# A graph layer on one core: gathers of 127 rows instead of 128, chunks of 508 edges

## The chip, the cores and the metric

The kernel runs on one core of a Trainium2 chip. A core has five engines that run their own instruction streams and meet at semaphores: TensorE (PE), VectorE (DVE), ScalarE (ACT), GpSimd (POOL) and SyncE (SP, which here only starts transfers). Sixteen DMA engines move data between the chip's memory (HBM) and the on-chip memory (SBUF, 128 partitions, called lanes here). The metric is the device time of one execution in microseconds.

## The reference, cut to what matters

One layer of a graph network on N = 6250 nodes of D = 256 features and E = 200000 edges, sorted by their destination node `dst`. The part that the change touches is the attention over the edges:

```python
xw = (x @ W).reshape(N, H, C)                  # H = 8 heads of C = 32
e = leaky_relu(a_src[src] + a_dst[dst], 0.2)
ex = exp(e - m[dst])                           # m: a bound per destination
denom = segment_sum(ex, dst, N)
msg = xw[src] * (ex / denom[dst])[:, :, None]
out = relu(segment_sum(msg, dst, N) + bias)
```

Beside it stand a second attention over all nodes (the "mix" part) and, behind both, a layer of 16 experts of which each node takes two.

## The kernel before

**Stages.** A setup (0 to about 50 us) builds tables; a keys stage (to about 370 us) goes over the nodes in 50 tiles of 128 and writes one row of ROW = 264 floats per node to the HBM tensor `node_rows` (its projected features and its 8 source logits); the edge loop (to about 3180 us) handles the edges; the experts and the last normalization follow.

**Chunks and steps.** The edges are cut into chunks of CHUNK = 512: four tiles of 128 edges, one edge per lane. The destinations are cut into 49 blocks of 128 nodes. A step handles one chunk against one block; since the edges are sorted, a chunk that reaches over a block's end is taken once more with the next block. That makes STEPS = CHUNKS + BLOCKS - 1 = 392 + 48 = 440 steps. Which chunk and block belong to a step is computed in the setup (`blk_row`, `need_row`, `first_row`).

**GpSimd** gathers. `gather` (line 205) starts four indirect transfers per chunk; each takes 128 rows of `node_rows`, one into each lane of `rows_g`, at the row numbers in `idx`. `rows_g` holds R = 4 chunks. Before a chunk's buffer is filled again, GpSimd waits on `msg_ready` for the last step that reads it (`last_use`, line 960). **SP** waits for each chunk's landing, counts it in `chunks_in` (line 985), and every four chunks loads their row numbers from `src_lists` into `idx` (line 215).

**VectorE**, in each step: builds the 0/1 matrix `sel` (line 1083), adds up the destination logits `ends` (1144), waits for the chunk and forms the logits `lg` (1150 to 1154), adds the sums of two steps ago from `p_m` to `acc` (1092), and multiplies the gathered features with the weights into `msg` (1161). **ScalarE** takes the exponentials (1059, 1061) and builds the matrix `sel_t` for three steps ahead (1011, 1014) out of `dst_all`, which an ACT-issued transfer fills for four steps at a time (222). **TensorE** spreads the destination logits (1183) and sums the messages per node (1193). Between these, the mix part runs as "query" work, spread over the steps (lines 1019 to 1037 on ScalarE, 1201 to 1252 on TensorE). The loop is unrolled on all of these engines.

**The lists.** `src_lists[p, chunk, u]` is the source node of the edge at lane p of tile u. SP writes it from `src` in 48 transfers of 8 chunks each during the keys stage (line 847), the last chunks in the setup (337 to 341). `dst_pad` is `dst` with padding, one row per chunk; `d_bf` are its rows per step, minus the block's first node, turned so that the lane is the inner index; an edge of another block or a padded one matches no node of the block.

Of the kernel before, what the change touches and what calls it, by code (L numbers as in the profile page):

```python
# [19 lines left out]
P = 128  # L20
N = 6250
E = 200000
# [8 lines left out]
CHUNK = TILES_PER_CHUNK * P  # L31
CHUNKS = 392
STEPS = CHUNKS + BLOCKS - 1
# [40 lines left out]
assert STEPS % OCT == 0 and GROUPS_Q * SPAN + OCT < STEPS and OCT % R == 0  # L74
assert LIST_TILES % 2 == 0 and LIST_TILES * LIST_CHUNKS <= E // CHUNK and CHUNKS % (2 * R) == 0 and CHUNKS * CHUNK >= E and CHUNKS == OCT * (T - 1)

# [54 lines left out]
def gps_layer(nc, x, src, dst, gnn_W, att_src, att_dst, gnn_bias, Wqkv, bqkv, Wproj, bproj, temperature,  # L131
# [12 lines left out]
    with top:  # L144
# [5 lines left out]
        dst_bc = nc.dram_tensor("dst_bc", (4 * P, CHUNK), BF16).ap()  # L150
# [85 lines left out]
        with ExitStack() as c:  # L236
# [29 lines left out]
            d_bf = [sb(f"d_bf{i}", [P, CHUNK], BF16, ctx=c) for i in range(G4)]  # L266
# [51 lines left out]
            def _(sp):  # L318
                full = E // CHUNK
                rest = E - full * CHUNK  # L320
                sp.dma_start(fd[:, 0:full], dst[0:full * CHUNK].rearrange("(c b) -> c b", b=CHUNK)[:, 0:1].rearrange("c a -> a c"),
                             allow_slow_non_contiguous=True).then_inc(first_in, 16)
                sp.dma_start(fd[:, full:full + 1], dst[full * CHUNK:full * CHUNK + 1].unsqueeze(0)).then_inc(first_in, 16)
                sp.dma_start(dst_pad[0:full, :], dst[0:full * CHUNK].rearrange("(a b) -> a b", b=CHUNK)).then_inc(dst_padded, 16)
# [14 lines left out]
                sp.dma_start(src_lists[:, lo:full, :], src[lo * CHUNK:full * CHUNK].rearrange("(a p u) -> p a u", p=P, u=u4)).then_inc(scratch_out, 16)  # L339
# [15 lines left out]
                sp.wait_ge(scratch_out, (2 + TQ - T + G4 + 1) * 16)  # L355

            @block.gpsimd
            def _(pool):
# [14 lines left out]
                pool.wait_ge(dst_padded, 4 * 16)  # L373
# [5 lines left out]
            def _(dve):  # L379
                dve.memset(resid[:, NFULL:T, :], 0.0).then_inc(x_zeroed, 1)  # L380
                dve.memset(att_bd[:], 0.0).then_inc(att_zeroed, 1)
                dve.memset(pad_s[:], 0).then_inc(pads_set, 1)
                dve.memset(pad_i[:], PAD_DST).then_inc(pads_set, 1)
# [26 lines left out]
                dve.wait_ge(first_in, 2 * 16)  # L410
# [132 lines left out]
        with ExitStack() as c:  # L543
# [1470 lines left out]
```

## Time and profile before

| | us |
|---|---|
| time, median of two runs | 3901.03 (3893.41 and 3908.66) |
| span of the profiled execution | 3964.1 |
| PE busy | 2866.8 (72%) |
| DVE busy | 2138.6 (54%) |
| POOL busy | 1990.0 (50%) |
| ACT busy | 1439.2 (36%) |
| software DMA queue (GpSimd's transfers) | 21.8% of 16 engines |

The profile is that of one execution. "Busy" counts the time in which an engine works on instructions other than register, branch, semaphore and transfer-starting ones; an indirect transfer on GpSimd counts, since GpSimd writes its list of pieces itself. "Idle before" a group of instructions is the engine's idle time just ahead of them, with the instruction whose semaphore ended it; "issue" means that the profile shows nothing that was waited for, and "remote" that the semaphore's writer is not among the records. A transfer's own time on the DMA engines is not part of the instruction that starts it.

### The profile page before, as it was taken

How to read it: one execution, taken by the hardware profiler on the slowest of the kernel's cores; microseconds unless marked ns; L12 is line 12 of the kernel's file. 1: busy time of each engine (PE TensorE's matmuls, PEld its weight loads, DVE VectorE, ACT ScalarE, POOL GpSimd, SP SyncE). 2: the span in 40 equal slices, each digit the busy share in tenths (PEclk: the TensorE clock that was granted, in tenths of full speed). 3: DMA queues.
4: the chain of work that ended last, by engine and by line, in shares of the span. 5: the costliest groups of instructions: out<-in, count | busy, mean ns of one | idle time of the engine just before them, and what ended most of it. 6: DMA issues, size and time to landing. Idle time of an engine off the chain costs nothing. (4 is left out here: it accounts for less than half of the span.)

```text
span 3964.1 us, 53285 instructions
## 1 busy us (share of the span) xinstructions
PE 2866.8 (72%) x12200; PEld 1793.8 (45%) x12200; DVE 2138.6 (54%) x5047; ACT 1439.2 (36%) x3425; POOL 1990.0 (50%) x2097
## 2 busy tenths in 40 slices
PE   5998776768677767676767675867685442599997
PEld 3554343434344333434343333333443332488885
DVE  7888545555555554545555555554555584333335
ACT  3444433334333334343434343433343221122226
POOL 3666554555555555555555555555555445222223
PEclk9999787878778788777877788878778755799999
DMA  5222333333333333333333333333333312677776
GB/s 140 44 44 62 108 97 92 100 101 101 101 102 106 96 105 99 105 97 105 97 96 97 109 93 104 99 104 99 98 96 105 89 39 82 205 233 232 233 232 222
DMA packets 298730, 453.14 MB, mean 114 GB/s; under 512 B 117295, under 2 KB 193348, under 8 KB 298479
## 3 DMA queue, kind: packets, MB, share of 16 engines
q0 software_dynamic: 86608, 243.35, 21.8%
q1 hardware_dynamic: 184143, 135.80, 12.5%
q10 hardware_dynamic: 27744, 71.38, 5.3%
q8 instruction: 83, 1.36, 0.1%
q14 instruction: 152, 1.25, 0.1%
HBM read 395.09 MB, written 56.88 MB: 114 GB/s over the span
## 5 line engine op out<-in xcount | busy, mean ns | idle before, releaser
L211 POOL DMA_INDIRECT rows_g<-node_rows,idx x1568 | 1488.3, 949 | 1293.4 <-DVE msg L1161 829.8
L1193 PE MATMUL p_m<-msg,sel 128*128 128x264 f32 x3520 | 1114.1, 469 | 292.5 <-DVE msg L1161 185.0
L1193 PEld LDWEIGHTS p_m<-msg,sel 128*128 128x128 f32 x3520 | 769.9, 230 | 447.7 <-issue 308.0
L1161 DVE TENSOR_TENSOR msg<-rows_g,p_w 128x1024 f32<-128x1024 f32 x440 | 536.2, 1219 | 345.6 <-ACT p_w L1059 228.9
L1037 ACT ACTIVATE qfeat<-p_scr 128x512 f32<-128x512 f32 x442 | 245.0, 593 | 798.9 <-remote 603.2
L1216 PE MATMUL p_scr<-q_t,sel_sum 32*128 32x512 f32 x832 | 340.9, 774 | 221.0 <-ACT qfeat L1037 177.1
L1083 DVE TENSOR_TENSOR sel<-p_w,dst_t 128x512 f32<-128x512 f32 x441 | 304.3, 690 | 139.0 <-issue 114.9
L1092 DVE TENSOR_TENSOR acc<-acc,p_m 128x264 f32 x440 | 189.0, 429 | 311.4 <-remote 280.6
L1014 ACT ACTIVATE sel_t<-apart,ones 128x512 bf16<-128x512 bf16 x443 | 319.7, 722 | 31.3 <-issue 1.1
L1011 ACT ACTIVATE apart<-dst_all,iota_neg 128x512 bf16<-128x512 bf16 x443 | 314.1, 709 | 0.0
L1845 POOL DMA_INDIRECT moe<-ysb,token x128 | 123.7, 966 | 379.2 <-DVE ysb L1834 354.9
L1059 ACT ACTIVATE p_w<-lg 128x32 f32<-128x32 f32 x440 | 88.4, 201 | 575.2 <-DVE lg L1154 451.7
L1183 PEld LDWEIGHTS p_sp<-adm_parts,sel_t 128*128 128x128 bf16 x1768 | 99.7, 103 | 428.4 <-issue 419.3
L1216 PEld LDWEIGHTS p_scr<-q_t,sel_sum 32*128 32x128 f32 x832 | 97.9, 219 | 367.2 <-issue 331.4
L1800 ACT ACTIVATE ht<-e_ph,ba 128x256 f32<-128x256 f32 x256 | 100.3, 474 | 415.7 <-PE e_ph L1770 409.9
L1770 PE MATMUL e_ph<-xst,wa 128*128 128x256 f32 x1024 | 234.0, 382 | 3.6 <-DMA bb<-in_L_ffn_b_dram 1.9
L1224 PE MATMUL p_y<-qfeat,mix_w 128*32 128x512 f32 x832 | 170.7, 686 | 88.3 <-ACT qfeat L1037 73.8
L540 POOL TENSOR_TENSOR acc<-kk 128x512 f32<-128x512 f32 x150 | 167.7, 1147 | 131.2 <-DVE kk L773 131.2
L1779 PE MATMUL e_py<-wb,ht 128*128 128x256 f32 x1024 | 231.4, 379 | 0.0
L1144 DVE TENSOR_REDUCE ends<-p_sp 128x64 f32<-128x192 f32 x440 | 153.6, 349 | 136.5 <-remote 119.7
L1183 PE MATMUL p_sp<-adm_parts,sel_t 128*128 x1768 | 127.8, 193 | 115.0 <-DVE lg L1154 80.8
L1770 PEld LDWEIGHTS e_ph<-xst,wa 128*128 128x128 f32 x1024 | 195.8, 192 | 31.9 <-issue 5.0
(328 smaller groups left out, 3375.6 us busy)
## 6 DMA issues: line engine op xcount, KB each, us to landing
dst_all<-dst_bc ACTq DMA_DIRECT2D x112, 512.0 KB
wa<-in_L_ffn_w_dram SPq DMA_DIRECT2D x64, 512.0 KB
wb<-in_L_ffn_w_dram SPq DMA_DIRECT2D x64, 512.0 KB
rows_g<-node_rows,idx POOLq DMA_INDIRECT x1568
xs<-slot_x SPq DMA_DIRECT2D x64, 258.0 KB
ya<-moe SPq DMA_DIRECT2D x48, 256.0 KB, 4.3
bb<-in_L_ffn_b_dram SPq DMA_DIRECT2D x64, 128.0 KB
qs<-xn_turned ACTq DMA_DIRECT2D x13, 512.0 KB
```

Source lines behind the costliest of these rows:

```text
L211: pool.indirect_dma_start(rows_g[:, j, u, :], None, node_rows, bass.IndirectOffsetOnAxis(ap=idx[q][:, j, u:u + 1], axis=0)).then_inc(gathe ...
L1011: act.activation(apart[j % 2][:], dst_all[q][:, j, :], ACT.Square, bias=iota_neg[:])
L1014: act.activation(sel_t[j][:], apart[j % 2][:], ACT.Relu, bias=ones[:, 0:1], scale=-1.0).then_inc(sel_t_ready, 1)
L1037: act.activation(feat[slot(name)][:], bank(name)[:], ACT.Square).then_inc(act_freed, 1)
L1083: dve.tensor_tensor(sel[j][:], p_w[:, P:2 * P].unsqueeze(1).broadcast_to([P, TC, P]), d.unsqueeze(2).broadcast_to([P, TC, P]), ALU.is_equa ...
L1092: dve.tensor_tensor(a, a, p_m[j % 2][:, 0:ROW], ALU.add).then_inc(acc_added, 1)
L1161: dve.tensor_tensor(m4, g3[:, :, 0:D].rearrange("p u (h e) -> p u h e", h=H), p_w[:, 0:TC * H].rearrange("p (u h) -> p u h", u=TC).unsquee ...
L1183: mm = pe.matmul(p_e(j)[:, u * 6 * H:(u + 1) * 6 * H], sel_t[j][:, u * P:(u + 1) * P], adm_parts[:, bass.ds(b, 1), :, :].rearrange("p a r ...
L1193: mm = pe.matmul(p_m[j % 2][:, 0:ROW], sel[j][:, u, :], msg[j % 2][:, u, :], start=(u == 0), stop=(u == TC - 1))
L1216: pe.matmul(bank(name)[:], sel_sum[rows, m * P:(m + 1) * P], q_t[g][rows, :], start=True, stop=True).then_inc(act_filled, 1)
L1770: mm = pe.matmul(p_h[s % 2][:, m * SLOT_ROWS:(m + 1) * SLOT_ROWS], wa[s][:, k, m * P:(m + 1) * P], xst[s % 2][:, k, :], start=(k == 0), st ...
L1779: mm = pe.matmul(p_y[s % 2][:, a * D:(a + 1) * D], ht[s % 2][:, k, a * P:(a + 1) * P], wb[s][:, k, :], start=(k == 0), stop=(k == KF - 1))
```

## The change

An indirect transfer takes 127 rows into lanes 0 to 126; lane 127 carries no edge. A chunk has four tiles of 127 edges, 508 in all, so the 200000 edges fill 394 chunks (FILLED; tables and lists are laid out for CHUNKS = 396), and there are 394 + 48 = 442 steps. Everything else in a step keeps its 128 lanes. Lane 127 has its own values: its destinations are NO_DST = -64, which matches no node, its row numbers are 0, and the lanes 96 to 127 of `rows_g` are set to zero once at the start of the keys stage. The loops on GpSimd and SP now end at chunk 394 and not at a multiple of 8. The lists are written with the chunk as outer index, and transfers over 393 full chunks are cut in two, at 384.

```diff
-CHUNK = TILES_PER_CHUNK * P
-CHUNKS = 392
-STEPS = CHUNKS + BLOCKS - 1
+LANES = 127
+CHUNK = TILES_PER_CHUNK * LANES
+FILLED = -(-E // CHUNK)
+CHUNKS = 396
+STEPS = FILLED + BLOCKS - 1
+WIDE = TILES_PER_CHUNK * P
+NO_DST = -64.0
...
             for u in range(TC):
-                pool.indirect_dma_start(rows_g[:, j, u, :], None, node_rows,
-                                        bass.IndirectOffsetOnAxis(ap=idx[q][:, j, u:u + 1], axis=0)).then_inc(gathered[j], 16)
+                pool.indirect_dma_start(rows_g[0:LANES, j, u, :], None, node_rows,
+                                        bass.IndirectOffsetOnAxis(ap=idx[q][0:LANES, j, u:u + 1], axis=0)).then_inc(gathered[j], 16)
...
+                even = full - full % 16
+                for lo, hi in ((0, even), (even, full)):
+                    sp.dma_start(fd[:, lo:hi], dst[lo * CHUNK:hi * CHUNK].rearrange("(c b) -> c b", b=CHUNK)[:, 0:1].rearrange("c a -> a c"),
+                                 allow_slow_non_contiguous=True).then_inc(first_in, 16)
...
+                for p in range(LANES, P):
+                    sp.dma_start(src_lists[p:p + 1, 0:full, :].rearrange("p a u -> p (a u)").rearrange("p (a b) -> (p a) b", a=u4),
+                                 pad_s[0:u4, 0:full]).then_inc(scratch_out, 16)
...
+                for g in range(G4):
+                    dve.memset(d_bf[g][:], NO_DST)
...
-                    dve.tensor_scalar(d_bf[g][:].rearrange("c (u p) -> c u p", u=TILES_PER_CHUNK),
+                    dve.tensor_scalar(d_bf[g][:].rearrange("c (u p) -> c u p", u=TILES_PER_CHUNK)[:, :, 0:LANES],
...
                 dve.memset(zeros[:], 0.0)
+                dve.memset(rows_g[P - C:P].rearrange("p r u f -> p (r u f)"), 0.0)
...
-                    sp.dma_start(src_lists[:, bass.ts(t, LIST_CHUNKS), :],
-                                 src[bass.ts(t, LIST_CHUNKS * CHUNK)].rearrange("(a p u) -> p a u", p=P, u=TILES_PER_CHUNK)).then_inc(lists_out, 16)
+                    sp.dma_start(src_lists[0:LANES, bass.ts(t, LIST_CHUNKS), :].rearrange("p a u -> a p u"),
+                                 src[bass.ts(t, LIST_CHUNKS * CHUNK)].rearrange("(a p u) -> a p u", p=LANES, u=TILES_PER_CHUNK)).then_inc(lists_out, 16)
```

On GpSimd, the place where the keys stage ends and the edge loop begins, before (three chunks are gathered ahead of the loop, then groups of four with a table lookup for each):

```order
L211 DMA rows_g<-node_rows,idx 128x264 x12
L543 UNCONDITIONAL_BRANCH
L958 UNCONDITIONAL_BRANCH
L211 DMA rows_g<-node_rows,idx 128x264 x4
L962 TENSOR_LOAD tables
L962 ISA x2
```

And the same place now:

```order
L215 DMA rows_g<-node_rows,idx 127x264 x12
L556 UNCONDITIONAL_BRANCH
L972 UNCONDITIONAL_BRANCH
L215 DMA rows_g<-node_rows,idx 127x264 x4
L976 TENSOR_LOAD tables
L976 ISA x2
```

Nothing has moved there; each transfer has 127 rows of 264 floats. On SP, the first transfers of the setup before, up to the last list:

```order
L321 DMA fd<-in_dst_dram 1x390x1
L323 DMA fd<-in_dst_dram 1x1
L324 DMA dst_pad<-in_dst_dram 16x12480
L325 DMA dst_pad<-in_dst_dram 16x20
L327 DMA dst_pad<-pad_i 1x192
L328 DMA dst_pad<-pad_i 1x512
L332 DMA resid<-in_x_dram 128x12x256 x4
L334 DMA resid<-in_x_dram 106x256
L337 DMA src_lists<-pad_s 128x8
L339 DMA src_lists<-in_src_dram 128x6x4
L341 DMA src_lists<-in_src_dram 80x4
```

And the same place now:

```order
L327 DMA fd<-in_dst_dram 1x384x1
L327 DMA fd<-in_dst_dram 1x9x1
L329 DMA fd<-in_dst_dram 1x1
L331 DMA dst_pad<-in_dst_dram 16x12192
L331 DMA dst_pad<-in_dst_dram 12x381
L332 DMA dst_pad<-in_dst_dram 4x89
L334 DMA dst_pad<-pad_i 1x152
L335 DMA dst_pad<-pad_i 2x508
L339 DMA resid<-in_x_dram 128x12x256 x4
L341 DMA resid<-in_x_dram 106x256
L344 DMA src_lists<-pad_s 128x12
L346 DMA src_lists<-in_src_dram 9x127x4
```

There are three more transfers in the setup, two of them in these rows and one for lane 127 of the lists behind them, and the lists' outer index is now the chunk.

## Rows read from the trace of the kernel before

**Rows 1.** The page, 40 equal slices of the span, busy tenths.

```profile
PE   5998776768677767676767675867685442599997
DVE  7888545555555554545555555554555584333335
POOL 3666554555555555555555555555555445222223
DMA  5222333333333333333333333333333312677776
```

**Rows 2.** Busy time in two stretches (clock, DMA share, GB/s last).

```profile
100.00:360.00 260.00, 255.38 (x1406) 134.56 (x1402) 223.96 (x537) 126.33 (x413) 180.53 (x206) 1.00 0.24 45
...
500.00:3100.00 2600.00, 1826.12 (x7130) 1031.74 (x7130) 1377.51 (x3020) 996.52 (x2216) 1386.14 (x1462) 0.80 0.35 100
```

**Rows 3.** By source line: ns min/median/max, first and last start in us.

```profile
L211 POOL DMA_INDIRECT rows_g<-node_rows,idx x1568: 940/946/1413, 376.0 to 3156.6; - x196
...
L1161 DVE TENSOR_TENSOR msg<-rows_g,p_w x440: 1206/1220/1223, 400.9 to 3172.8; 128x1024 f32<-128x1024 f32 x147
```

**Rows 4.** The page, costliest groups: busy us, mean ns, idle before.

```profile
L211 POOL DMA_INDIRECT rows_g<-node_rows,idx x1568 | 1488.3, 949 | 1293.4 <-DVE msg L1161 829.8
```

**Rows 5.** Timeline of two pauses (start, length, idle before).

```profile
1848.25 0.94 POOL L211 DMA_INDIRECT rows_g<-node_rows,idx  x1 [0.30 <-issue]
1849.50 0.95 POOL L211 DMA_INDIRECT rows_g<-node_rows,idx  x1 [0.30 <-issue]
...
1853.85 0.69 DVE L1083 TENSOR_TENSOR sel<-p_w,dst_t 128x512 f32<-128x512 f32 x1 [6.71 <-issue]
...
1854.51 0.95 POOL L211 DMA_INDIRECT rows_g<-node_rows,idx  x1 [0.30 <-issue]
1858.14 0.19 DVE L1150 TENSOR_TENSOR lg<-rows_g,ends 128x32 f32<-128x32 f32 x1 [3.34 <-issue]
1858.21 1.08 ACT L1037 ACTIVATE qfeat<-p_scr 128x512 f32<-128x512 f32 x2 [11.60 <-remote]
...
1898.79 0.95 POOL L211 DMA_INDIRECT rows_g<-node_rows,idx  x1 [0.30 <-issue]
1902.14 0.69 ACT L1030 ACTIVATE r_norm<-p_scr,c_col 128x512 f32<-128x512 f32 x1 [10.77 <-remote]
```

**Rows 6.** Waits of the whole span: us in total, times, longest.

```profile
POOL rows_g L211 <- DVE msg L1161: 829.8, 186, 10.8
```

**Rows 7.** Timeline of two undisturbed steps on VectorE.

```profile
1790.11 1.21 DVE L1161 TENSOR_TENSOR msg<-rows_g,p_w 128x1024 f32<-128x1024 f32 x1
...
1793.69 1.22 DVE L1161 TENSOR_TENSOR msg<-rows_g,p_w 128x1024 f32<-128x1024 f32 x1
```

**Rows 8.** Windows of 2 us at the second pause.

```profile
1899.00:1901.00 2.00, 0.00 (x0) 0.00 (x0) 0.02 (x1) 0.00 (x0) 0.74 (x1) 0.50 0.50 133
1901.00:1903.00 2.00, 0.12 (x1) 0.12 (x1) 0.00 (x0) 0.78 (x2) 0.00 (x0) 0.50 0.01 2
```

**Rows 9.** Register instructions of VectorE's sequencer, by source line.

```profile
L1150 DVEq ALU_OP  x880: 1/45/1422, 398.4 to 3171.3; - x176
...
L1139 DVEq SEQ_ASSERT  x440: 5/23/729, 395.5 to 3170.2; - x147
```

**Rows 10.** Transfers that GpSimd starts, with their counts.

```profile
rows_g<-node_rows,idx POOLq DMA_INDIRECT x1568
...
moe<-ysb,token POOLq DMA_INDIRECT x128
...
slot_x<-acc,places POOLq DMA_INDIRECT x98
...
d_rows<-dst_pad,cidx POOLq DMA_INDIRECT x4, 6.5
```

**Rows 11.** The software queue: packets, MB, share of 16 engines.

```profile
q0 software_dynamic: 86608, 243.35, 21.8%
```

**Rows 12.** Two memsets of VectorE, by source line.

```profile
L382 DVE MEMSET pad_s<- x1: 485/485/485, 1.6 to 1.6; 128x512 int32 x1
...
L407 DVE MEMSET acc<- x1: 4232/4232/4232, 6.6 to 6.6; 128x5008 f32 x1
```

**Rows 13.** VectorE at the setup's end and the keys stage's start.

```profile
46.86 0.17 DVE L463 TENSOR_SCALAR t_col<-t_col 128x2 f32<-128x2 f32 x1 [3.81 <-DMA bq_col<-in_L_mix_bqkv_dram]
...
58.51 0.15 DVE L750 COPY mask<-vmask 128x1 f32<-128x1 f32 x1 [1.39 <-PE p_kv L689]
```

**Rows 14.** The list transfers: issue times, and landing.

```profile
L847 SPq DMA_DIRECT2D src_lists<-in_src_dram x48: 585/622/1592, 59.5 to 355.1; - x48
...
DMA to landing us min/median/max: 5.8/6.7/8.6
```

More of the change, by code:

```diff
@@ L73 @@
 WEIGH_STEPS = ((7, 9, 12, 15), (19, 21, 23, 25))
-assert STEPS % OCT == 0 and GROUPS_Q * SPAN + OCT < STEPS and OCT % R == 0
-assert LIST_TILES % 2 == 0 and LIST_TILES * LIST_CHUNKS <= E // CHUNK and CHUNKS % (2 * R) == 0 and CHUNKS * CHUNK >= E and CHUNKS == OCT * (T - 1)
+assert GROUPS_Q * SPAN + OCT < STEPS and OCT % R == 0
+assert LIST_TILES % 2 == 0 and LIST_TILES * LIST_CHUNKS <= E // CHUNK and CHUNKS % R == 0 and CHUNKS - R < FILLED < CHUNKS and STEPS + 2 * R <= 4 * P
 def wait(eng, sem, value):
@@ L265, in gps_layer @@
             ident_bf = sb("ident_bf", [P, P], BF16, ctx=c)
-            d_bf = [sb(f"d_bf{i}", [P, CHUNK], BF16, ctx=c) for i in range(G4)]
+            d_bf = [sb(f"d_bf{i}", [P, WIDE], BF16, ctx=c) for i in range(G4)]
             p_g = ps("p_g", [P, 512], c)
@@ L320, in _ @@
                 rest = E - full * CHUNK
-                sp.dma_start(fd[:, 0:full], dst[0:full * CHUNK].rearrange("(c b) -> c b", b=CHUNK)[:, 0:1].rearrange("c a -> a c"),
-                             allow_slow_non_contiguous=True).then_inc(first_in, 16)
+                even = full - full % 16
+                for lo, hi in ((0, even), (even, full)):
+                    sp.dma_start(fd[:, lo:hi], dst[lo * CHUNK:hi * CHUNK].rearrange("(c b) -> c b", b=CHUNK)[:, 0:1].rearrange("c a -> a c"),
+                                 allow_slow_non_contiguous=True).then_inc(first_in, 16)
                 sp.dma_start(fd[:, full:full + 1], dst[full * CHUNK:full * CHUNK + 1].unsqueeze(0)).then_inc(first_in, 16)
-                sp.dma_start(dst_pad[0:full, :], dst[0:full * CHUNK].rearrange("(a b) -> a b", b=CHUNK)).then_inc(dst_padded, 16)
+                for lo, hi in ((0, even), (even, full)):
+                    sp.dma_start(dst_pad[lo:hi, :], dst[lo * CHUNK:hi * CHUNK].rearrange("(a b) -> a b", b=CHUNK)).then_inc(dst_padded, 16)
                 sp.dma_start(dst_pad[full:full + 1, 0:rest], dst[full * CHUNK:E].unsqueeze(0)).then_inc(dst_padded, 16)
@@ L974, in _ @@
                     body(R + j, 1, j, done[j])
-                for i in range(1, CHUNKS // (2 * R)):
-                    for q in range(2):
-                        done = [last_use(i * (2 * R) + q * R + j) for j in range(R)]
-                        for j in range(R):
-                            body(i * (2 * R) + q * R + j, q, j, done[j])
+                for i in range(2, CHUNKS // R):
+                    js = range(min(R, FILLED - i * R))
+                    done = [last_use(i * R + j) for j in js]
+                    for j in js:
+                        body(i * R + j, i % 2, j, done[j])
             @block.sync
@@ L985, in arrived @@
                     sp.sem_inc(chunks_in, 1)
-                def body(ch, q, more):
-                    for j in range(R):
+                for ch in range(0, CHUNKS, R):
+                    for j in range(min(R, FILLED - ch)):
                         arrived(ch + j, j)
-                    if more:
-                        fetch_lists(sp, ch + 2 * R, q)
-                body(0, 0, True)
-                body(R, 1, True)
-                for i in range(1, CHUNKS // (2 * R) - 1):
-                    for q in range(2):
-                        body(i * (2 * R) + q * R, q, True)
-                for q in range(2):
-                    body(CHUNKS - (2 - q) * R, q, False)
+                    if ch + 2 * R < CHUNKS:
+                        fetch_lists(sp, ch + 2 * R, ch // R % 2)
             @block.scalar
@@ L1073, in _ @@
                 for q in range(2):
-                    act.wait_ge(dst_in[q], (STEPS // R // 2 + 1) * 16)
+                    act.wait_ge(dst_in[q], (1 + len(range(1 + q * R, STEPS, 2 * R))) * 16)
                 act.wait_ge(q_in, GROUPS_Q * 16)
```

11 lines of the change are left out of this document (6 added, 5 removed).

## Prediction, made before the changed kernel ran

> **What bounds the kernel now.** I read the 40 slices of the page first [rows 1], then the busy time in two long windows [rows 2]. From 500 to 3100 us no engine is full: TensorE is busy 0.70 of the time, VectorE 0.53, GpSimd 0.53, ScalarE 0.38, and the DMA engines 0.35. The keys stage (100 to 360 us) is different: PE is busy 0.98 of it. So the loop over steps waits on something, and it takes most of the program: the 440 multiplies `msg` of line 1161 start from 400.9 to 3172.8 us [rows 3], 6.3 us per step.
>
> GpSimd's account explains the length of the loop. It starts its 1568 gathers from 376.0 to 3156.6 us, 2781 us [rows 3]. One gather occupies it 0.949 us on average [rows 4], and back to back they start 1.25 us apart (1848.25 to 1849.50 us in [rows 5]), so a chunk of four costs 5.0 us and all of them 1568 x 1.25 = 1960 us. The rest is waiting for `msg` to free a buffer: 829.8 us in 186 waits, the longest 10.8 us [rows 6]. 1960 + 830 = 2790 us, the loop to within 0.4%. So loop = gathers x 1.25 + W, where W is what GpSimd waits for the other engines.
>
> Are the other engines slow by their own work? No. Two successive `msg` start 3.6 us apart when nothing disturbs them (1790.11 and 1793.69 us, [rows 7]), less than the 5.0 us of a chunk. W comes from pauses. In [rows 5] GpSimd runs seven gathers without a break while ScalarE does nothing for 11.60 us and VectorE waits 6.71 us with "issue" as releaser, which means that no semaphore explains it. Both go on at 1858.14 and 1858.21 us, 2.7 us after the end of the last gather's issue (1854.51 + 0.95). The second pause reads the same: last gather 1898.79 + 0.95 = 1899.74 us, ScalarE back at 1902.14 us after 10.77 us. The windows beside it show why I connect the two: DMA share 0.50 from 1899 to 1901 us, 0.01 from 1901 to 1903 us, and the engines come back in the quiet window [rows 8]. VectorE's sequencer shows it from inside: register instructions of line 1150 with a median of 45 ns take up to 1422 ns, an assertion of 23 ns up to 729 ns [rows 9]. Something that every sequencer needs is withheld while gathers are in flight, and is given back when GpSimd has filled its four chunk buffers and must stop. I do not know from these rows what it is; I only use when it ends.
>
> **What a gather does to the DMA engines.** The software queue moved 86608 packets for 1568 + 128 + 98 + 4 indirect transfers and 3 plain ones [rows 10, 11], 48 packets for each: 3 for each of 16 engines. So 128 rows are split evenly, 8 to an engine, and all 16 engines serve every gather at once.
>
> **The change, part by part.**
> 1. 127 rows instead of 128. 127 is prime; if the split must stay even, all rows go to one engine. Price of the transfer: the queue's 243.35 MB took 21.8% of 16 engines' span [rows 11], 0.218 x 16 x 3964 = 13826 us, 17.6 KB per us of one engine. 127 rows of 1056 bytes are 134 KB, 7.6 us on one engine, where sixteenths take about 0.5 us. Hidden: a buffer is refilled in 5.0 us of issue, lands at most 7.6 us later, and is read by about 3.6 us of step, 16.2 us against the 4 x 5.0 = 20 us that four buffers give. The cover is 3.8 us; if the engines serve a gather slower than 11 us, VectorE waits for rows.
> 2. What it does to the pauses. No row shows a gather that uses one engine, so W is bounded from both sides: 0 if the pauses go, 830 if nothing changes, and 830 + 186 x 7 = 2130 if each wait lasts as long as the longer tail of the last gather. I take half of W, 415 us. The reason for a gain rather than a loss: a pause needs traffic that keeps all 16 DMA engines supplied from GpSimd; with one engine per gather about six of sixteen are in use (7.6 / 1.25), and whatever the sequencers fetch or write has free engines in between. The reason for only half: the DMA engines are idle for two thirds of the loop already (share 0.35), and the gaps between two gathers don't end a pause now, so it is not a matter of full DMA engines alone.
> 3. GpSimd's issue of one gather. It covers the same number of rows, so I take 1.25 us. Bounds by the nearest rows: 0.940 to 1.413 us busy for gathers of this kind [rows 3], so -0.01 to +0.46 us on each of 1576, -10 to +730 us; I take the median because 1568 of them agree with it.
> 4. Size. 1576 gathers instead of 1568: +10 us. Two more steps without query work: already inside the formula, since loop = gathers x 1.25 + W; as steps they would be 2 x 6.3 = 12.6 us with pauses, 2 x 3.6 without. I take +10 for both.
> 5. Setup. Four more memsets of 128x512 on VectorE, at most 485 ns each (the 4-byte one of line 382, [rows 12]), +1.9 us; hidden in part by the 3.81 us that VectorE waits for `bq_col` [rows 13], but SP then issues three more transfers of 0.4 to 0.6 us in that same stretch. +2 us together. The memset of lanes 96 to 127 of `rows_g` is 4224 elements long; 5008 took 4232 ns [rows 12], so 3.6 us, at the place where VectorE waits only 1.39 us for the first projection [rows 13]: +2.2 us.
> 6. Source lists. 48 transfers are cut 8 x 127 x 4 instead of 128 x 8 x 4, so on 8 engines instead of 16 and about twice as long. Now one lands 6.7 us after issue [rows 14]; doubled it is 13.4 us against a whole stage of about 300 us, and only `fetch_lists` at its end waits for them. The last one starts at 355.1 us and the first gather at 376.0 us [rows 3, 14], so 20.9 - 6.7 = 14 us cover the extra 6.7 us. 0 us; without that cover +7 us.
>
> Sum: -415 + 10 + 2 + 2 = -401 us. The profiled execution has a span of 3964 us, the two timed runs 3893 and 3909 us with a median of 3901; the profiled one is 1.6% longer, and I carry the difference over: 3964 - 401 = 3563 us of span, 3500 us timed.
>
> Here a page speaks for point 1. The Trainium skill, "DMA: Bandwidth & Descriptors", section "Why a DMA increments its semaphore by 16 and not by 1", says that a transfer runs on the largest number of engines up to 16 that divides its outermost dimension, and gives 127 partitions as the case with one; on GpSimd's queue successive transfers move round the engines. The same section lists an exception, direct copies from GpSimd that spread 127 partitions over all 16. The trace agrees with the even split of 128 (48 packets each) and shows neither case for 127.
>
> **The rivals.**
> - Nothing changes (the split stays on 16 engines, or moves and the pauses don't care). For: 7 or 8 rows per engine is an easy split, and the pauses may hang on the number of rows in flight. W stays 830: 3901 + 14 = 3915 us. The exception named above would give this.
> - Slower, longer pauses. For: in both pauses shown the engines return only after the traffic has stopped, and on one engine it stops up to 7 us later. It decides against the change as soon as the pauses do not thin out. The waits have a mean of 4.5 us and a longest of 10.8; my estimate is that some 70 of the 186 are long ones of 6 us and more, and if these grow by 7 us each it is +490 us, 4400 us.
> - Slower, the issue. For: writing 127 rows' worth of descriptors for one engine may be serial. From 1.25 + 830/1576 = 1.78 us per gather on, GpSimd alone makes the loop as long as now, whatever the pauses do. At 2.5 us: 3940 us of loop, +1150, 5050 us. Against: no indirect transfer in the trace, of rows of 1 to 2 KB, takes more than about 1.4 us.
> - All gathers on the same engine: 1576 x 7.6 = 11980 us. Only if the engine were fixed; the trace has no sign of one.
>
> **How the numbers follow.** One engine and thinner pauses 0.43 (3500 us, its own range 3090 to 3820: W gone or nearly kept); one engine, pauses as now 0.09; still 16 engines 0.17 (both 3915 us); longer pauses 0.20 (3915 to 4400 us, of which a quarter below 3980); dearer issue 0.10 (3700 to 5050 us); fixed engine 0.01. The range 3090 to 4400 us leaves out about 0.15. A measurement of this kernel can tell about 2% from no change, so faster means below 3823 us: 0.43 + 0.02 = 0.45. Within 2%: 0.09 + 0.17 = 0.26 less what drifts out, plus the small end of the longer pauses, 0.25. Slower: 0.30.
>
> **What would show it.** Step 1: packets per gather and the time from the end of issue to landing; if a chunk still arrives 1 to 2 us after its last issue, all 16 engines serve it. Step 2: GpSimd's wait for `msg`, 415 us; 829.8 again means the pauses stay, over 1200 the tail matters. Step 3: mean of the gather's busy time, 0.95 us; above 1.4 us the issue has become the bound, and the wait for `msg` would vanish. Steps 5 and 6: the keys stage starts at most 5 us later and lasts as long as before. I am wrong from the ground up if the waits vanish and the loop is not shorter, or if VectorE's `lg` starts to wait for rows.

## Result, and the profile after

The changed kernel takes 5773.04 us (median of two runs, 5769.27 and 5776.81), against 3901.03 us before: a ratio of 1.479, 95% interval 1.470 to 1.487. The prediction was 3500 us with a range of 3090 to 4400 us. The time lies outside it, on the other side of no change.

The profiled execution of after has a span of 5775.0 us. In the table below, all of the growth is in the edge loop.

| us | before | after |
|---|---|---|
| span | 3964.1 | 5775.0 |
| first gather starts | 376.0 | 378.1 |
| first to last gather | 2780.6 | 4606.7 |
| from the last gather's start to the end | 807.5 | 790.2 |
| gathers | 1568 | 1576 |
| GpSimd busy with one gather | 0.949 | 2.541 |
| GpSimd's wait for `msg` | 829.8 | 17.0 |

The page of after, 40 slices (answers to [rows 1]); GpSimd now stands at 8 tenths through the whole loop, and VectorE fell from 5 tenths to 3:

```profile
PE   6975545455555555455555545555555543348998
DVE  8863333333333333333323332332323233553334
POOL 4778888888888888888888888888888888662223
DMA  4223333323233333333333333333333333227776
```

The same stretch as the second row of [rows 2], with the same columns:

```profile
500.00:3100.00 2600.00, 1392.10 (x4391) 787.84 (x4390) 832.42 (x1843) 606.88 (x1358) 2262.06 (x891) 0.67 0.31 64
```

GpSimd is busy 2262 of 2600 us (before: 1386) and does 891 things in that time where it did 1462. The gather by its source line, its group on the page, and the software queue (answers to [rows 3, 4, 11]):

```profile
L215 POOL DMA_INDIRECT rows_g<-node_rows,idx x1576: 2530/2540/2952, 378.1 to 4984.8; - x197
...
L215 POOL DMA_INDIRECT rows_g<-node_rows,idx x1576 | 4004.1, 2541 | 605.3 <-issue 588.3
...
q0 software_dynamic: 843408, 254.77, 22.4%
```

No gather takes less than 2.53 us. The queue's packets went from 86608 [rows 11] to 843408. The 230 other indirect transfers keep about 48 each, so a 127-row gather has (843408 - 230 x 48) / 1576 = 528 packets instead of 48. The waits of the whole span (answers to [rows 6]):

```profile
DVE lg L1156 <- SPq L999: 2814.4, 391, 11.0
...
POOL rows_g L215 <- DVE msg L1167: 17.0, 23, 1.1
```

The roles have changed. GpSimd hardly waits for `msg` any more (17.0 us instead of 829.8), and VectorE waits 2814.4 us for rows to arrive. The loop is GpSimd's own work: (4004.1 + 605.3 - 17.0) / 1576 = 2.914 us per gather, 1576 x 2.914 = 4592 us, plus the 17.

What became of the pauses is in VectorE's register instructions at `lg`, where [rows 9] had 1422 ns as the maximum:

```profile
L1156 DVEq ALU_OP  x884: 40/45/52, 424.4 to 4995.7; - x177
```

From 1 to 1422 ns around the median of 45 the spread has shrunk to 40 to 52. The stall inside the sequencers is gone. So half of the prediction came true, and something else, larger, went wrong.

The start of the gathers in the timeline of after says whether the 2.54 us are GpSimd's own:

```profile
378.12 2.63 POOL L215 DMA_INDIRECT rows_g<-node_rows,idx  x1 [0.18 <-issue]
381.06 2.54 POOL L215 DMA_INDIRECT rows_g<-node_rows,idx  x1 [0.30 <-issue]
```

The first gather of the program takes 2.63 us with no other gather in flight. It isn't held back by the ones before it.

### The profile page after: what moved, and what is told of

Read it like the earlier page. It is cut to its first block and busy times, and to the rows that moved or that the text cites. A ratio compares the mean times of both kernels' runs of the same rounds, so it can differ in the third digit from the quotient of the medians.

```text
span 5775.0 us, 53429 instructions
## 1 busy us (share of the span) xinstructions
PE 3339.7 (58%) x12224; PEld 2068.9 (36%) x12224; DVE 2139.6 (37%) x5066; ACT 1435.7 (25%) x3433; POOL 4507.9 (78%) x2105
## 2 busy tenths in 40 slices
DMA packets 1055435, 465.10 MB, mean 81 GB/s; under 512 B 873663, under 2 KB 949734, under 8 KB 1055184
## 3 DMA queue, kind: packets, MB, share of 16 engines
q0 software_dynamic: 843408, 254.77, 22.4%
q14 instruction: 152, 1.25, 0.1%
## 5 line engine op out<-in xcount | busy, mean ns | idle before, releaser
L215 POOL DMA_INDIRECT rows_g<-node_rows,idx x1576 | 4004.1, 2541 | 605.3 <-issue 588.3
L1199 PE MATMUL p_m<-msg,sel 128*128 128x264 f32 x3536 | 1539.4, 609 | 513.7 <-DVE msg L1167 505.9
L1199 PEld LDWEIGHTS p_m<-msg,sel 128*128 128x128 f32 x3536 | 1027.3, 305 | 791.1 <-issue 549.2
L1156 DVE TENSOR_TENSOR lg<-rows_g,ends 128x32 f32<-128x32 f32 x442 | 84.9, 192 | 2832.7 <-SPq L999 2814.4
L1189 PE MATMUL p_sp<-adm_parts,sel_t 128*128 x1776 | 140.5, 206 | 1506.7 <-DVE lg L1160 1477.4
L1222 PE MATMUL p_scr<-q_t,sel_sum 32*128 32x512 f32 x832 | 325.9, 780 | 102.2 <-DVE q_gram L1118 102.2
L1785 PEld LDWEIGHTS e_py<-wb,ht 128*128 128x128 f32 x1024 | 189.7, 190 | 23.2
```

Source lines behind the costliest of these rows:

```text
L215: pool.indirect_dma_start(rows_g[0:LANES, j, u, :], None, node_rows, bass.IndirectOffsetOnAxis(ap=idx[q][0:LANES, j, u:u + 1], axis=0)).th ...
L1189: mm = pe.matmul(p_e(j)[:, u * 6 * H:(u + 1) * 6 * H], sel_t[j][:, u * P:(u + 1) * P], adm_parts[:, bass.ds(b, 1), :, :].rearrange("p a r ...
L1199: mm = pe.matmul(p_m[j % 2][:, 0:ROW], sel[j][:, u, :], msg[j % 2][:, u, :], start=(u == 0), stop=(u == TC - 1))
L1222: pe.matmul(bank(name)[:], sel_sum[rows, m * P:(m + 1) * P], q_t[g][rows, :], start=True, stop=True).then_inc(act_filled, 1)
L1785: mm = pe.matmul(p_y[s % 2][:, a * D:(a + 1) * D], ht[s % 2][:, k, a * P:(a + 1) * P], wb[s][:, k, :], start=(k == 0), stop=(k == KF - 1))
```

## The experiments

In the diffs below a line with - is of the kernel named, and only the lines that matter are shown. Two theories of the loss were open (the row count by itself, or something else in the change), then three rules for how the row count acts, and then two for the pauses: K, they need a gather on (nearly) all 16 engines, as the prediction said; and P, they need gathers that follow each other closely, at 1.25 us or little more.

### The row count alone, and everything but the row count

**e1**, from the kernel before:

```diff
+GATHER = 127
...
-                pool.indirect_dma_start(rows_g[:, j, u, :], None, node_rows,
+                pool.indirect_dma_start(rows_g[0:GATHER, j, u, :], None, node_rows,
```

> The kernel before (chunks of 512 edges, 440 steps, lists as before); only the gathers take 127 rows, and lanes 96 to 127 of rows_g are zeroed once. The 128th edge of each tile is left out. Theory (the gather's row count is the whole cause): the gather stays busy 2.54 us and starts 2.84 us apart, the loop takes 1568 x 2.92 = 4580 us, total 5700 to 5770 us. Rival (the cause lies in the new lists, the new chunk size or the lane-127 data): the gather goes back to 0.95 us and the total to 3900 to 3950 us.

**e2**, from the changed kernel:

```diff
-                pool.indirect_dma_start(rows_g[0:LANES, j, u, :], None, node_rows,
+                pool.indirect_dma_start(rows_g[:, j, u, :], None, node_rows,
```

> The changed kernel (chunks of 508, 442 steps, new lists and setup) with the gather alone put back to 128 rows; lane 127 then fetches row 0 of node_rows, which matches no destination. Theory (the row count is the whole cause): gather busy 0.95 us, pauses and wait for msg as before (830 us, give or take 60), total 3901 + 14 = 3915 us, ratio 1.00 to 1.01. Rival (the rest of the change costs something by itself): above 3960 us, with a longer keys stage or a longer wait for idx.

e1 took 5750.2 us (one run; before on the same chip 3905.9), e2 3927.7 us, a ratio of 1.006 (1.004 to 1.008). Their groups on the page, e1 first:

```profile
L212 POOL DMA_INDIRECT rows_g<-node_rows,idx x1568 | 3987.9, 2543 | 597.0 <-issue 585.1
```

```profile
L215 POOL DMA_INDIRECT rows_g<-node_rows,idx x1576 | 1496.2, 949 | 1254.0 <-DVE msg L1167 785.9
```

One row less in each gather makes up 1844 of the 1872 us lost. Chunks of 508, two more steps, the new lists and the setup cost 22 us together (0.6%).

### How the row count acts

**e3, e4, e5 and e6** are e1 with 124, 122, 126 and 120 in the place of 127. Like e1 they leave out edges (those of the missing lanes), so they measure time only; the steps and the number of gathers are those of the kernel before.

> The kernel before with gathers of 124 rows (4 x 31); the last four edges of each tile are left out. Theory A: a gather uses the largest number of engines up to 16 that divides its rows (4 engines, 31 rows each, 8 packets of up to 4 rows) and every one of the 16 queues gets as many entries as the fullest, 8 x 16 = 128; issue time is linear in entries between the two cases measured (32 entries 0.949 us, 512 entries 2.541 us): 1.27 us busy, 1.57 us apart, 2460 us for all, plus what GpSimd waits for msg: total 3570 us if the pauses go, 3990 us if half of them stay, 4400 us if all stay. Theory B: every count that is not a multiple of 16 is written row by row at about 20 ns a row: 2.48 us busy, total 5600 us. Theory C (only prime or odd counts are special): as before, 0.93 us busy, total 3900 us.

> The kernel before with gathers of 122 rows (2 x 61); the last six edges of each tile are left out. Theory A (largest divisor up to 16, here 2; 61 rows on each, 16 packets, 256 entries): 1.69 us busy, 1.99 us apart, 3120 us for all plus the wait for msg: total 4230 us if the pauses are gone, up to 4700 if half stay. Theory B (all counts that are no multiple of 16 alike): 2.44 us busy, total 5500 us. Theory C (only odd counts): 0.92 us, total 3900 us.

> The kernel before with gathers of 126 rows (14 x 9); the last two edges of each tile are left out. Entries by the divisor rule: 14 engines, 9 rows each, 3 packets, 3 x 16 = 48 entries (blank ones on two engines only), issue 0.95 to 1.0 us, 1.30 us apart, 2040 us for all. Theory K (the pauses need a gather on all 16 engines; 4 engines had none): the wait for msg nearly vanishes, the loop is 2040 to 2150 us, total 3150 to 3300 us. Rival P (the pauses were thinned by the slower pace of 1.6 us and not by fewer engines): wait for msg about 800 us as before, total 3850 to 3950 us.

> The kernel before with gathers of 120 rows (15 x 8); the last eight edges of each tile are left out. Entries by the divisor rule: 15 engines, 8 rows each, 2 packets, 32 entries, so the issue time is that of 128 rows, 0.95 us (a cost per row would give 0.89). Theory K (pauses need all 16 engines): one free engine is enough, wait for msg under 150 us, total 3050 to 3250 us. Rival P (pace): wait for msg 700 to 830 us, total 3800 to 3900 us.

Measured: e3 3667.9 us (ratio 0.939, 0.936 to 0.941), e4 4251.9 us (one run), e5 3875.8 us (0.990, 0.986 to 0.993), e6 3894.8 us (0.994, 0.992 to 0.997). Group and software queue of e3, e4 and e5, in that order:

```profile
L212 POOL DMA_INDIRECT rows_g<-node_rows,idx x1568 | 2024.4, 1291 | 483.7 <-issue 456.5
...
q0 software_dynamic: 237136, 239.06, 26.2%
```

```profile
L212 POOL DMA_INDIRECT rows_g<-node_rows,idx x1568 | 2606.4, 1662 | 483.5 <-issue 461.5
...
q0 software_dynamic: 437840, 238.78, 23.7%
```

```profile
L212 POOL DMA_INDIRECT rows_g<-node_rows,idx x1568 | 1553.3, 991 | 1152.3 <-DVE msg L1163 692.4
...
q0 software_dynamic: 111696, 240.16, 22.8%
```

Theories B (no multiple of 16: all alike) and C (only odd counts) are out: 124 and 122 are both even and no multiples of 16, and cost 1.29 and 1.66 us. Theory A gave 1.27 and 1.69. The Trainium skill, "DMA: Bandwidth & Descriptors", section "Why a DMA increments its semaphore by 16 and not by 1", says that the largest number up to 16 that divides the outermost dimension is the number of engines; the runs agree with it for indirect transfers by their packets and issue times. Its exception for direct copies does not hold for them: 127 rows did not spread over 16 engines.

**e13** asks whether GpSimd writes for 2.54 us or waits for the one engine that moves the rows.

```diff
-                pool.indirect_dma_start(rows_g[:, j, u, :], None, node_rows,
+                pool.indirect_dma_start(rows_g[0:GATHER, j, u, 0:ROW // 2], None, node_rows.rearrange("n (a f) -> (n a) f", a=2),
```

> The kernel before with gathers of 127 rows, each row half as long (132 floats from a view of the same table; the other half of every gathered row and the 128th edge of each tile are left out, so the output means nothing). The number of entries per gather stays 512, the bytes halve. Theory (GpSimd's own writing of entries sets the 2.54 us): issue 2.5 us as before, total 5700 to 5770 us. Rival (GpSimd is held back by the one engine that moves the rows, 5 us a gather): the issue falls towards 1.3 to 1.9 us, total 3900 to 4700 us.

5639.4 us (one run). Its group and queue:

```profile
L212 POOL DMA_INDIRECT rows_g<-node_rows,idx x1568 | 3987.4, 2543 | 483.7 <-issue 479.1
...
q0 software_dynamic: 437840, 148.50, 14.4%
```

With half the bytes the gather still costs 2.543 us, so GpSimd is not held up by the moving of the bytes. That it is GpSimd's own writing is what is left; the first gather above, 2.63 us with nothing in flight, says the same. The expectation missed one thing, and it is instructive. It said that the entries (which I counted as packets) stay at 512, but the packets halved too (272 per gather instead of 528). So the time does not go with packets. What stayed the same is the number of rows on the one engine. With r the rows on each engine that takes part:

| rows | engines | r | busy us | 0.84 + 0.0134 r |
|---|---|---|---|---|
| 128 | 16 | 8 | 0.949 | 0.95 |
| 120 (e6) | 15 | 8 | 0.976 | 0.95 |
| 126 (e5) | 14 | 9 | 0.991 | 0.96 |
| 121 (e12) | 11 | 11 | 1.019 | 0.99 |
| 119 (e11) | 7 | 17 | 1.098 | 1.07 |
| 125 (e18) | 5 | 25 | 1.204 | 1.18 |
| 124 (e3) | 4 | 31 | 1.291 | 1.26 |
| 122 (e4) | 2 | 61 | 1.662 | 1.66 |
| 127 (e1) | 1 | 127 | 2.543 | 2.54 |

The line goes through the first and the last value ((2.541 - 0.949) / 119 = 0.0134 us a row) and misses the others by less than 0.04 us. The packets per gather, worked out for each run as for after, are 48, 64, 64, 96, 128, 144, 272 and 528 for r = 8, 9, 11, 17, 25, 31, 61 and 127: always 16 + 16 x r/4, r/4 rounded up (with the half rows of e13 it is r/8). So each of the 16 queues gets as many packets as the fullest one; of a 127-row gather 15 x 32 = 480 packets carry no rows. The packet sizes bear this out. The page's line for all queues, before and after:

```profile
DMA packets 298730, 453.14 MB, mean 114 GB/s; under 512 B 117295, under 2 KB 193348, under 8 KB 298479
...
DMA packets 1055435, 465.10 MB, mean 81 GB/s; under 512 B 873663, under 2 KB 949734, under 8 KB 1055184
```

873663 - 117295 = 756368 more packets are shorter than half a row, and 480 x 1576 = 756480. In the trace of after 732840 packets of the software queue have 16 bytes and 23640 have 12, together exactly that number: four bytes for each of the 127 rows that the full queue has. In e13 these packets are half as many and have 32 and 28 bytes, again four for each of 127 rows. So what a gather has in each queue, full or blank, goes with r, and so does GpSimd's time.

### What the pauses depend on

e5 and e6 already spoke against K: with 14 and 15 engines the wait for `msg` was 692.4 and 728.7 us, where K wanted nearly nothing. But at 4 engines (e3) it was 27.2 us. e3 also came at a slower pace. The next runs vary the pace alone.

**e7 and e8**, from the kernel before (e8 has the added pair twice):

```diff
                                         bass.IndirectOffsetOnAxis(ap=idx[q][:, j, u:u + 1], axis=0)).then_inc(gathered[j], 16)
+                pool.memset(pace[:], 0.0)
+                pool.drain()
```

> The kernel before, complete, 128-row gathers on 16 engines; GpSimd sets a small tile of 48 floats per lane and drains after each gather, which spaces the gathers at about 1.45 to 1.55 us instead of 1.25. Rival P (the pauses come from the pace of 1.25 us): they go, loop 1568 x 1.5 = 2350 us, total 3460 us. Theory K (they come from gathers on all 16 engines): they stay, the wait for msg falls only by the part that the slower pace hides, total 3900 to 4100 us.

> As the run with one such pair, with two pairs of set and drain after each gather, gathers 1.65 to 1.8 us apart, at least the 1.59 us of the 124-row gathers. Rival P (pace): no pauses, wait for msg under 60 us, loop 1568 x 1.7 = 2670 us, total 3780 us. Theory K (engines): pauses stay, longest gaps of 6 us and more on ScalarE and TensorE, total 3950 to 4200 us.

7114.1 us (ratio 1.815, 1.810 to 1.821) and 7532.2 us (1.923, 1.917 to 1.928): the drain costs far more than I had assumed, so they say nothing on where a limit lies. They show one thing: all 16 engines serve each gather (86608 packets, as before), and yet no register instruction at `lg` exceeds 52 ns. GpSimd's timeline in e7:

```profile
2002.18 0.95 POOL L212 DMA_INDIRECT rows_g<-node_rows,idx  x1 [2.49 <-issue]
2003.13 0.15 POOL L215 MEMSET pace<- 128x48 f32 x1
2005.77 0.95 POOL L212 DMA_INDIRECT rows_g<-node_rows,idx  x1 [2.48 <-issue]
```

After the tile is set GpSimd stands still for 2.5 us until the next gather. e7 still shows 337 us of waits for `msg` (70, the longest 5.3 us). They are hardly real. From 2000 to 4000 us 21 gaps of 4.8 to 5.3 us at chunk ends are put down to `msg`, but 14 others of 4.4 to 5.2 us name nothing that was waited for, so the gap is as long without it, and VectorE is ahead, for it waits 4303.6 us for rows. The 279.7 us of e8 were not examined.

**e9 and e10** replace the drain by a wait on the semaphore that the tile's own instruction raises (e10: two tiles after each gather).

```diff
+                    pool.wait_ge(gather_opened, opened[0])
+                    pool.memset(pace[:], 0.0).then_inc(gather_opened, 1)
+                    opened[0] += 1
```

> The kernel before, complete, 128-row gathers on 16 engines; after each gather GpSimd sets one tile of 48 floats per lane (no drain), with a semaphore of its own between them, which spaces the gathers at about 1.45 us. Theory P (the pauses come from the pace of 1.25 us, not from the number of engines): they thin out or go, wait for msg below 300 us, total 3400 to 3700 us. Theory K (they go when a gather uses few engines, as with 4 and 2, and 14 or 15 are not few): they stay; total 3850 to 4000 us.

> As the run before with two such tiles set after each gather, gathers about 1.6 to 1.7 us apart, the pace at which 124-row gathers on 4 engines had no pauses (1.59 us). Theory P: no pauses, wait for msg under 60 us, loop 1568 x 1.65 = 2590 us, total 3700 us. Theory K: pauses stay, TensorE and ScalarE together idle for 3 us and more some 100 times, total above 3900 us.

e9: 3932.2 us (0.990, 0.984 to 0.995). Its gathers were only 1.26 us apart in a chunk, since one tile fits into the 0.30 us between two gathers, so it tested little. e10: 3879.2 us (0.978, 0.973 to 0.983). VectorE's register instructions at `lg`, and GpSimd's wait:

```profile
L1157 DVEq ALU_OP  x880: 40/45/52, 402.5 to 3079.1; - x176
...
POOL rows_g L214 <- issue: 480.3, 402, 3.1
POOL rows_g L214 <- DVE msg L1168: 5.8, 2, 2.9
```

All 16 engines serve each gather, and there are no pauses. So gathers on 16 engines are not enough to make pauses. The time fell little (3700 us was expected) because the waits also keep GpSimd from reading its tables ahead: 480 us of idle at the chunk ends bring the average to 1.72 us per gather.

**e11 and e12** are the changed kernel, complete, with another number of lanes.

```diff
-LANES = 127
+LANES = 119
-CHUNKS = 396
+CHUNKS = 424
```

(e12: 121 and 416.)

> The changed kernel, complete, with 119 lanes (7 x 17) instead of 127: chunks of 476 edges, 421 chunks, 469 steps, 1684 gathers. Divisor rule: 7 engines, 17 rows each, 5 packets, 80 entries, issue 1.10 us, 1.40 us apart, 2360 us for all. Theory K: 7 engines are few enough, wait for msg under 100 us, total 3480 to 3560 us. Theory P: at 1.40 us apart about half of the pauses stay, wait for msg 300 to 600 us, total 3750 to 4050 us.

> The changed kernel, complete, with 121 lanes (11 x 11): chunks of 484 edges, 414 chunks, 462 steps, 1656 gathers. Divisor rule: 11 engines, 11 rows each, 3 packets, 48 entries, issue 0.99 us, 1.29 us apart, 2140 us for all. Theory K with a limit above 11 engines: total 3260 to 3400 us; with a limit below 11: as 14 and 15 engines, wait for msg about 700 us, total 3950 us. Theory P: as that last one, about 3950 us.

4040.3 us (1.018, 1.011 to 1.025) and 4099.9 us (1.034, 1.028 to 1.039); waits for `msg` 460.8 and 694.0 us. Seven and eleven engines still have pauses. So K is refuted from both sides: pauses come without 16 engines, and 16 engines come without pauses (e10).

**e14 and e15** set three and four one-byte slots after each gather, with no wait that binds. **e17** sets the tile of e10 three times, but not after a chunk's last gather, so that GpSimd can look ahead there.

```diff
+                for i in range(3):
+                    k = (calls[0] % 8 * TC + u) * 3 + i
+                    pool.memset(pace[:, k:k + 1], 0).then_inc(gather_opened, 1)
```

```diff
+                for _ in range(3 if u < TC - 1 else 0):
+                    pool.wait_ge(gather_opened, opened[0])
+                    pool.memset(pace[:], 0.0).then_inc(gather_opened, 1)
+                    opened[0] += 1
```

> The kernel before, complete, 128-row gathers on 16 engines; after each gather GpSimd sets three one-byte slots of a tile (about 0.11 us each), and waits on none of them within the next four chunks, so that it can look ahead over the chunk's end. Gathers about 1.45 us apart throughout. Theory P (pace, limit at or below 1.45 us): wait for msg under 100 us, loop 1568 x 1.45 = 2270 to 2370 us, total 3370 to 3480 us. Theory P with a limit above: pauses as in the kernel with 119 lanes (1.40 us apart), total 3700 to 3950 us. Theory K (few engines needed): pauses stay, total 3850 us or more.

> As the run before with four slots set after each gather, about 1.55 us apart. Theory P: no pauses, wait for msg under 60 us, loop 1568 x 1.55 = 2430 to 2480 us, total 3530 to 3600 us. Theory K: pauses stay, total above 3850 us.

> The kernel before, complete, 128-row gathers on 16 engines; after the first three gathers of each chunk, and not after the fourth, GpSimd sets a tile of 48 floats three times, each after a wait for the one before: three gathers 1.65 us apart and one 1.25, 6.2 us a chunk, 1.55 us on average, and GpSimd can look ahead over the chunk's end. Theory P (pace): wait for msg under 100 us, loop 392 x 6.2 = 2430 to 2530 us, total 3530 to 3650 us against 3900 to 3960. Theory K (engines): pauses stay, total above 3800 us.

3911.3 us (0.986, 0.982 to 0.989), 3839.5 us (0.968, 0.963 to 0.974) and 3764.8 us (0.951, 0.948 to 0.954). The small slots gave 1.27 and 1.30 us inside a chunk and not the 1.45 and 1.55 that I had written, so both expectations failed (no pauses, 3370 to 3480 and 3530 to 3600 us). e17 lost its pauses as P says, but with 1.65 us per gather on average instead of 1.55 it missed the 3530 to 3650 us. VectorE's register instructions in e15, then in e17:

```profile
L1162 DVEq ALU_OP  x880: 6/45/709, 401.0 to 3042.3; - x176
```

```profile
L1157 DVEq ALU_OP  x880: 40/45/52, 402.4 to 2974.5; - x176
```

Inside a chunk the gathers of e10 and those of e15 follow each other like this:

```profile
1801.17 0.95 POOL L214 DMA_INDIRECT rows_g<-node_rows,idx  x1
1802.62 0.95 POOL L214 DMA_INDIRECT rows_g<-node_rows,idx  x1
```

```profile
1800.86 0.95 POOL L218 DMA_INDIRECT rows_g<-node_rows,idx  x1
1802.15 0.95 POOL L218 DMA_INDIRECT rows_g<-node_rows,idx  x1
```

All runs in one table. Pace is GpSimd's time per gather without the wait for `msg`: (busy + idle of the group, with the pacing tiles - wait) / gathers; for the kernel before that is (1488.3 + 1293.4 - 829.8) / 1568 = 1.24 us [rows 4]. It is an average that holds the gaps at the chunk ends too. "Inside" is the median distance from one gather's start to the next between 1000 and 2600 us, mostly within chunks. Loop is first to last gather.

| run | engines | pace us | inside us | wait for `msg` us | loop us | longest register instruction at `lg`, ns |
|---|---|---|---|---|---|---|
| before | 16 | 1.24 | 1.25 | 829.8 | 2781 | 1422 |
| e2 | 16 | 1.25 | 1.25 | 785.9 | 2749 | 708 |
| e6 | 15 | 1.27 | 1.28 | 728.7 | 2722 | 717 |
| e5 | 14 | 1.28 | 1.30 | 692.4 | 2704 | 1393 |
| e12 | 11 | 1.31 | 1.32 | 694.0 | 2870 | 1393 |
| e9 | 16 | 1.34 | 1.26 | 658.5 | 2752 | 728 |
| e14 | 16 | 1.40 | 1.27 | 544.0 | 2737 | 725 |
| e11 | 7 | 1.42 | 1.40 | 460.8 | 2854 | 729 |
| e15 | 16 | 1.45 | 1.30 | 393.8 | 2658 | 709 |
| e18 | 5 | 1.50 | 1.51 | 16.6 | 2419 | 52 |
| e16 | 4 | 1.58 | 1.59 | 31.1 | 2575 | 52 |
| e3 | 4 | 1.58 | 1.59 | 27.2 | 2507 | 52 |
| e17 | 16 | 1.65 | 1.64 | 7.7 | 2596 | 52 |
| e10 | 16 | 1.72 | 1.45 | 5.8 | 2700 | 52 |
| e4 | 2 | 1.96 | 1.96 | 21.9 | 3088 | 52 |
| e13 | 1 | 2.85 | 2.85 | 4.6 | 4468 | 52 |
| after | 1 | 2.91 | 2.85 | 17.0 | 4607 | 52 |
| e1 | 1 | 2.92 | 2.85 | 11.9 | 4582 | 52 |
| e7 | 16 | 3.58 | 3.61 | 337.0 (see above) | 5953 | 52 |
| e8 | 16 | 3.89 | 3.86 | 279.7 (see above) | 6374 | 52 |

Read by engines the wait has no order: 16 stands at 830 and at 6. Read by pace it falls with hardly an exception up to 1.45 us, and from 1.50 us on it is small and the long register instructions are gone. The amount of data does not order it: e11 and e18 both gather 88 KB per us of pace (119 and 125 rows of 1056 bytes), and they wait 460.8 and 16.6 us; nor do the packets, of which e18 has 128 per gather and the kernel before 48. Up to 1.45 us the loop takes about 2650 to 2870 us whatever GpSimd does: the other engines, with their pauses, set it. From 1.50 us on the loop is gathers x pace, and the same other engines do their steps in 2419 us, which they could not do in any run with pauses. So in this kernel the pauses stop at a pace between 1.45 and 1.50 us, and every microsecond of pace beyond that is lost again.

How far this goes must be said. The two runs beside that limit differ in engines too: e15 has 16, e18 has 5. With 16 engines alone the limit lies between 1.45 us (e15) and 1.65 us (e17) on average, and inside a chunk between 1.30 us (e15) and 1.45 us (e10, whose gathers stop for a while at the chunk ends). Part of the average of e15 is itself a stall: 40.9 us in 12 gaps, the longest 9.5 us, end with GpSimd's own sequencer. No run has five engines or fewer at a pace under 1.50 us, so that the number of engines shifts the limit is neither shown nor excluded.

### Kernels that use both rules

**e16** is the changed kernel with 124 lanes (CHUNKS = 408), **e18** with 125. 400 chunks of 500 edges are exactly the 200000, so the last chunk's padding transfer goes:

```diff
-LANES = 127
+LANES = 125
-CHUNKS = 396
+CHUNKS = 404
...
-                full = E // CHUNK
+                full = (E - 1) // CHUNK
```

> The changed kernel, complete, with 124 lanes (4 x 31): chunks of 496 edges, 404 chunks, 452 steps, 1616 gathers, 4 engines a gather, 128 entries, issue 1.29 us. From the run with 124-row gathers on the old chunks (3668 us, 1568 gathers, no pauses): 48 gathers more at 1.60 us, +77 us, total 3745 us, 3700 to 3800. Should the list transfers or the steps matter by themselves, above 3800 us.

> The changed kernel, complete, with 125 lanes (5 x 25): chunks of 500 edges, 400 chunks, 448 steps, 1600 gathers; 5 engines, 25 rows each, 7 packets, 112 entries; issue 1.23 us between the 1.10 us of 80 entries and the 1.29 us of 128, so 1.53 us apart, 2450 us for all. If the pauses are gone at this pace: wait for msg under 60 us, total 3640 to 3690 us, 2 to 3% below the kernel with 124 lanes. If they come back below 1.55 us: wait for msg over 150 us and no gain over 124 lanes.

e16: 3780.0 us (0.954, 0.951 to 0.957), inside its range. e18: 3599.5 us against 3961.0 us on the same chip, a ratio of 0.909 (0.907 to 0.912), complete and with 8 steps and 32 gathers more than before; that is better than the 3640 to 3690 us expected, with the gathers 1.50 us apart and not 1.53. Its group and waits:

```profile
L215 POOL DMA_INDIRECT rows_g<-node_rows,idx x1600 | 1926.5, 1204 | 494.3 <-issue 477.8 <-DVE msg L1166 16.6
...
DVE lg L1155 <- SPq L998: 270.5, 101, 6.6
```

In e18 GpSimd and the rest are nearly in balance: GpSimd waits 16.6 us for `msg`, VectorE 270.5 us for rows. Both are faster than the kernel before although each of their gathers takes GpSimd longer.

## Why the prediction was wrong

**What bounds the kernel (right).** The formula loop = gathers x own time + W is GpSimd's account, so it holds for every run by the way the own time is counted; with the measured one it gives the result: 1576 x 2.914 + 17 = 4609 us against 4606.7. What the runs add is which of the two terms gives way: W is nearly zero as soon as the pauses are gone. One reading was too good: the 3.6 us between two `msg` in [rows 7] is a fast step. TensorE's busy share of 0.70 [rows 2] in steps of 6.3 us makes 4.4 us of its work per step, still less than the 5.0 us of a chunk.

**Point 1, all rows on one engine (right).** e3, e4, e5 and e11 follow the divisor, and 127 has only 1. The gathers can't all be on the same engine: a gather's 134 KB at 17.6 KB/us are an estimated 7.6 us on one engine, and gathers follow at 2.9 us. The arrival was sized a little too small. In the timeline of after, on GpSimd and VectorE:

```profile
2709.63 2.54 POOL L215 DMA_INDIRECT rows_g<-node_rows,idx  x1 [0.31 <-issue]
...
2721.66 0.19 DVE L1156 TENSOR_TENSOR lg<-rows_g,ends 128x32 f32<-128x32 f32 x1 [8.59 <-SPq L999]
```

The first line is the fourth gather of a chunk. `lg` starts 9.5 us after the end of its issue, not the 7.6 us assumed; the median over the chunks from 1000 to 2000 us is 8.4 us. That costs nothing here, for GpSimd is not held up by it (17.0 us of wait).

**Point 2, the pauses thin out (right in direction, wrong in reason).** I took 415 us as the gain; it was 829.8 - 17.0 = 813 us, the far bound. The reason given, free DMA engines, is refuted by e10 and e17 (16 engines, no pauses) and by e11 and e12 (7 and 11 engines, pauses). What the runs point to is the time between gathers, and in this kernel the change slowed them for another reason. That the pauses went was luck as far as the prediction goes.

**Point 3, issue 1.25 us (the step that failed).** "It covers the same number of rows, so I take 1.25 us", with a bound of +730 us. It measured 2.914 us per gather, of which GpSimd is busy 2.541 instead of 0.949: (2.914 - 1.245) x 1576 = +2630 us. The error is in what I counted. All 1568 gathers and all other indirect transfers of the trace were split evenly over 16 engines, so total rows and rows per engine were in one fixed ratio, and no row could tell them apart. The bound from the slowest gather (1.413 us) was a spread of the same shape, no bound for another one. Point 1 had just multiplied the rows on one engine by 16, and I did not ask what that does to the engine that writes the lists.

**Points 4 to 6 (right in sum).** e2 puts all of them together at +22 us (14 to 30), where they were given as 14. One by one they were not measured; the first gather starts 2.1 us later in after and 4.1 us later in e2, where +4 was given.

**The sum.** -401 us forecast. Measured in the profiled executions: -813 us of wait, +2630 us of issue and +10 us for eight more gathers are +1827, against 4606.7 - 2780.6 = +1826 us of loop.

**The rivals.** The third, "dearer issue", was the one that happened, given 0.10, though even its range ended at 5050 us. Its place was right, its crossover (1.78 us) fits the runs beside it (e10 at 1.72 us is faster than before, e4 at 1.96 us slower), and the prediction named the sign that decides: wait for `msg` vanished, busy above 1.4 us. Its example of 2.5 us (5050 us) was too low; at 2.91 us the same working gives 3901 - 2790 + 4609 = 5720 us. "Longer pauses" did not happen. "Nothing changes" was excluded by the packets. The sentence on being wrong from the ground up (the waits vanish and the loop is not shorter, `lg` waits for rows) describes the profile after word for word.

## What to carry to other kernels

Before the number of rows in a GpSimd gather is changed, factor it: in the nine counts tried here the largest divisor up to 16 is the number of engines, and GpSimd's own time goes with the rows on the fullest of them, not with the total. When the evidence for a price comes from instructions of one shape only, its spread is no bound for another shape; multiply through every quantity that the new shape changes. And when all engines stall at once while one of them issues transfers at full speed, try slowing that one: here 1.50 us between gathers instead of 1.24 (e18, 125 rows on 5 engines) made the kernel 9% faster, and 1.65 us with 128 rows on 16 engines (e17) made it 5% faster.

## What was unexpected in the hardware

- Blank packets: a gather on one engine puts as many packets into each of the other 15 queues, of 16 bytes at most. 86608 packets became 843408 for the same rows.
- The pauses end within a small step of pace: 393.8 us of waits at 1.45 us per gather (16 engines), 16.6 us at 1.50 us (5 engines). How much of this step is the pace alone, and which resource the sequencers wait for, is still open.
- A drain on GpSimd behind a gather stands for 2.5 us (e7), so it is no cheap spacer; small memsets vanish in the 0.30 us between two gathers (1.25 us apart without, 1.30 us with four of them).
- TensorE's mean granted clock fell from 0.80 to 0.67 of full speed in the stretch from 500 to 3100 us, as TensorE's busy share fell from 0.70 to 0.54. It cost nothing here, since GpSimd set the loop.
